# x1's scratch with 264 rows a channel, and the lifted operand loaded as four transfers of 24 partitions

## The reference

```
x = x + L0(gn(x))      # gn: group norm, 4 groups of 2 channels
x = x + L1(gn(x))
L0: 3x3 conv of 8 channels (centre tap masked) -> 32, relu, 1x1 conv -> 8
L1 (per group of 2 channels):
    h = fc0(concat(x, grid_x, grid_y))            # 1x1, 4 -> 10 per group: "the lift"
    for i in 0..3:
        h = irfft2(W_i * low modes of rfft2(h)) + conv1x1_i(h)
        if i < 3: h = h*sigmoid(softplus(beta_i)*h)/1.1
    h = fc2(swish(fc1(h)))                        # 10 -> 128 -> 2 per group
```

## Time and profile before

| | us |
|---|---|
| median of 3 runs | 23,844.61 |
| range of the 3 runs | 23,821.83 to 23,862.16 |
| the profiled execution | 23,827.96 |
| its span, first to last instruction | 23,826.2 |

### The profile page before, as it was taken

How to read it: one execution, slowest core, us unless ns; L and a number is a source line. 1 busy time by engine, 2 the same in 40 slices (tenths; PEclk the granted TensorE clock), 3 DMA queues, 4 the chain that set the end, 5 groups by cost and what they waited for, 6 DMA issues and landing times.

```text
span 23826.2 us, 590215 instructions
## 1 busy us (share of the span) xinstructions
PE 18081.9 (76%) x252434; PEld 7868.4 (33%) x252434; DVE 4542.3 (19%) x8917; ACT 13087.9 (55%) x16068; POOL 45.0 (0%) x69
## 2 busy tenths in 40 slices
PE   4787777787777877778777877777777778877778
PEld 2233332233332333333333333332333323333223
DVE  2111221112211122111121111211112211122111
ACT  2565445664455654556545655456554556544566
POOL 0000000000000000000000000000000000000000
PEclk8888888898888988889888888888888889888889
DMA  4333443334433344433444334443344433344333
GB/s 147 96 88 126 141 140 106 92 113 141 140 109 101 103 140 140 122 93 103 136 140 134 87 99 134 138 141 91 89 133 139 142 100 88 123 142 140 108 92 111
DMA packets 1497569, 2829.48 MB, mean 119 GB/s; under 512 B 126470, under 2 KB 395742, under 8 KB 1466986
## 3 DMA queue, kind: packets, MB, share of 16 engines
q1 hardware_dynamic: 1492353, 2789.18, 38.3%
q10 hardware_dynamic: 2408, 0.28, 0.0%
HBM read 1547.46 MB, written 1241.52 MB: 117 GB/s over the span
## 4 chain that ended last, share of the span: by engine, by line
PE 41%; DMA 26%; ACT 19%; DVE 7%; issue 5%; SPq 2%; ACTq 0%; DVEq 0%
PE PS L600 20%; ACT arena L705 18%; DMA h_d<-hmem 16%; DMA arena<-h_d 5%; DVE gst L904 4%; PE PS L498 4%; DMA hmem<-x_d 3%; PE PS L565 3%; PE PS L469 3%; PE PS L509 3%; PE PS L560 3%; PE PS L519 2%; DMA x_d<-arena 2%; PE PS L478 1%; PE PS L533 1%
## 5 line engine op out<-in xcount | busy, mean ns | idle before, releaser
L705 ACT ACTIVATE arena<-PS 128x1024 f32<-128x1024 f32 x8448 | 8186.8, 1021 | 1404.7 <-PE PS L600 1404.7
L600 PE MATMUL PS<-hmem,f1w 31*128 31x512 f32 x33792 | 4838.7, 642 | 541.9 <-DVE hmem L941 42.2
L613 PE MATMUL PS<-arena,f2w 128*32 128x512 f32 x33792 | 4511.4, 606 | 32.9 <-ACT arena L705 32.9
L565 PE MATMUL PS<-invc,gst 24*32 24x256 f32 x90112 | 3075.9, 421 | 218.4 <-issue 215.1
L698 ACT ACTIVATE hmem<-PS 128x2048 f32<-128x2048 f32 x1056 | 1982.8, 1878 | 1606.9 <-PE PS L565 1606.9
L600 PEld LDWEIGHTS PS<-hmem,f1w 31*128 31x128 f32 x33792 | 1327.0, 183 | 4312.1 <-ACT arena L705 4254.7
L498 PE MATMUL PS<-arena,fwdr 128*32 128x256 f32 x15360 | 1243.3, 450 | 1984.0 <-DMA arena<-h_d 1982.7
L666 ACT ACTIVATE arena<-PS 128x256 f32<-128x256 f32 x1024 | 392.4, 383 | 3956.3 <-PE PS L498 3956.3
L565 PEld LDWEIGHTS PS<-invc,gst 24*32 24x32 f32 x90112 | 2125.0, 144 | 1118.9 <-issue 890.1
L560 PE MATMUL PS<-hmem,mix 30*32 30x512 f32 x33792 | 1817.7, 657 | 440.8 <-DVE gst L904 347.8
L677 ACT ACTIVATE gst<-PS 24x264 f32<-24x264 f32 x2560 | 973.0, 380 | 1436.8 <-PE PS L533 1378.4
(11 more groups left out here) (105 smaller groups left out, 7605.1 us busy)
## 6 DMA issues: line engine op xcount, KB each, us to landing
arena<-h_d SPq DMA_DIRECT2D x960, 1024.0 KB, 6.8
h_d<-hmem SPq DMA_DIRECT2D x1408, 512.0 KB, 3.6
h_d<-hmem SPq DMA_DIRECT2D x1408, 256.0 KB, 4.0
shifted<-in_x SPq DMA_DIRECT2D x990, 128.0 KB
wspec<-in_spec_w SPq DMA_DIRECT2D x97, 1200.0 KB, 5.2
arena<-in_x SPq DMA_DIRECT2D x528, 128.0 KB, 2.5
x_d<-arena SPq DMA_DIRECT2D x512, 128.0 KB, 4.4
hmem<-x_d SPq DMA_DIRECT2D x128, 512.0 KB, 6.7
```

Of the source, the lines that this page charges most:

```text
L565: mm = nc.tensor.matmul(PS[32 * s:32 * s + 32, at + r, y * W:y * W + W], gst[32 * r:32 * r + MODES, s, :, 2 * u + y], invc[32 * r:32 * r + ...
L600: mm = nc.tensor.matmul(PS[:, 2 * ((2 * p + n) % 3) + r % 2, :], f1w[32 * r:32 * r + 31, k, g, :], hmem[32 * r:32 * r + 31, g * PART + u * ...
L613: mm = nc.tensor.matmul(PS[32 * c:32 * c + 32, 6 + u % 2, :], f2w[:, k, g, :], act[p % 2][:, c * ROW2:c * ROW2 + ROW2], start=kg == 0, sto ...
L705: nc.scalar.activation(act[p % 2][:, 1024 * n:1024 * n + 1024], PS[:, bank:bank + 2, :].rearrange("p a b -> p (a b)"), ACT.Silu).then_inc( ...
```

## The change

The scratch `x1_d` gets 264 rows a channel, so that 3 blocks of 88 rows fill it exactly. Rows 256 to 263 are cleared once, by one transfer of 8 partitions by 8 KB in the setup. With that, block k of channel ch begins at a fixed distance of 88 rows from the one before, over channels too. Chunk c of all 24 (channel, block) pairs is one transfer of 24 partitions by 22 rows, and the order within a partition group of 32 becomes channel first, block second (partition 32c + 3ch + k). All four are issued behind the second halves of the row images; no lift load is left between the stores.

The lift's weights in `liftt` are loaded in the new order of rows (three strided loads and one for the rest in place of one). The partitions of `lifted` now belong to other groups than those of the two layouts, so `gm` gets a third layout, each `group_sum` a third matmul, and POOL's power works on three columns. On DVE the two additions of EPS become one over three columns, and `lift_mean` is taken before POOL's power and not after. Addresses of the stores, the row images and the residuals use the new channel pitch (`X1_CH`).

```diff
-    to = np.stack([g, np.arange(128) // 32])
+    to = np.stack([g, np.arange(128) // 32, np.arange(128) % 32 // (NBLK * SC)])
...
-        x1_d = nc.dram_tensor("x1_d", [C, H, W], F32, kind="Internal")
+        x1_d = nc.dram_tensor("x1_d", [C, NBLK * KROWS, W], F32, kind="Internal")
...
-        LIFTED = 16 * (BLOCKS + 4)
+        LIFTED = 16 * (4 + 4)
+        X1_CH = NBLK * KROWS * W
...
-                  (liftt, lift_t[:, 0:32]), (liftb, lift_b), (lg, lift_g), (gridm, gridf), (mixb, mix_b),
+                  (liftt[:, CH - 16:32], lift_t[:, CH - 16:32]),
+                  *[(liftt[:, k:CH - 16:NBLK], lift_t[:, C * k:C * k + C]) for k in range(NBLK)], (liftb, lift_b), (lg, lift_g), (gridm, gridf), (mixb, mix_b),
...
-                def lift_rows(blocks):
-                    for c, k in blocks:
-                        p, n = 32 * c + C * k, kept(c, k, 0, PU)
-                        sp_.dma_start(lifted[p:p + C, 0:n * W], bass.AP(x1_d, (KROWS * k + YY * c) * W, [[PIX, C], [1, n * W]])
-                                      ).then_inc(s_lift, 16)
...
-                upper = [(c, k) for k in range(NBLK) for c in range(4) if KROWS * k + YY * c + YY <= H // 2]
                 for u in range(UNITS):
                     sp_.wait_ge(s_x1, i * UNITS + (u + 1 + HEAD_X1))
                     for t in (2 * u, 2 * u + 1):
-                        sp_.dma_start(combed(x1_d, NQ * t * W, NQ), xt[:, t * W:t * W + W]).then_inc(s_x1st[t // UNITS], 16)
+                        sp_.dma_start(combed(x1_d, NQ * t * W, NQ, X1_CH), xt[:, t * W:t * W + W]).then_inc(s_x1st[t // UNITS], 16)
                     if u == 4:
                         sp_.wait_ge(s_x1st[0], i * (16 * UNITS) + 16 * UNITS)
                         first_images(0)
-                        lift_rows(upper)
                 sp_.wait_ge(s_x1st[1], i * (16 * UNITS) + 16 * UNITS)
                 first_images(1)
-                lift_rows([(c, k) for k in range(NBLK) for c in range(4) if (c, k) not in upper])
+                for c in range(4):
+                    sp_.dma_start(lifted[32 * c:32 * c + NBLK * C, :], bass.AP(x1_d, YY * c * W, [[KROWS * W, NBLK * C], [1, PART]])
+                                  ).then_inc(s_lift, 16)
...
             sp_.wait_ge(s_set, SETUP_V)
+            sp_.dma_start(bass.AP(x1_d, PIX, [[X1_CH, C], [1, X1_CH - PIX]]), lifted[0:C, 0:X1_CH - PIX]).then_inc(s_pad, 16)
             for n in range(PARTS):
                 load(0, n)
+            sp_.wait_ge(s_pad, 16)
...
-                for layout in range(2):
+                for layout in range(3):
                     mm = nc.tensor.matmul(gnps[n][:, 2 * layout + r:2 * layout + r + 1], gm[:, layout, :], mv[:, 3 * r:3 * r + 1],
...
                 if n:
                     V.tensor_scalar(spectral_shift, gnps[n][:, 2:3], -1.0, None, ALU.mult)
-                    V.tensor_scalar(spectral_var, gnps[n][:, 3:4], EPS, None, ALU.add)
-                V.tensor_scalar(mv[:, 6:7], gnps[n][:, 1:2], EPS, None, ALU.add)
+                    V.tensor_scalar(lift_mean, gnps[n][:, 4:5], inside[:, 1:2], None, ALU.mult)
+                V.tensor_scalar(variances, gnps[n][:, 1:6:2], EPS, None, ALU.add)
                 V.drain().then_inc(s_var, 1)
                 dve.wait_ge(s_rstd, nth + 1)
                 if n:
-                    V.tensor_scalar(lift_mean, mean, inside[:, 1:2], None, ALU.mult)
-                    V.tensor_scalar(lift_rstd, rstd, inside[:, 1:2], inside[:, 2:3], ALU.mult, ALU.add)
+                    V.tensor_scalar(lift_rstd, row_rstd, inside[:, 1:2], inside[:, 2:3], ALU.mult, ALU.add)
...
-                nc.gpsimd.tensor_tensor(mv[:, 8:10], mv[:, 6:8], power[:, :], ALU.pow).then_inc(s_rstd, 1)
+                nc.gpsimd.tensor_tensor(rstds, variances, power[:, :], ALU.pow).then_inc(s_rstd, 1)
```

More of the change, by code:

```diff
@@ L178, in program @@
         mix13 = sb("mix13", [128, 2, 32]); mix2 = sb("mix2", [128, G, 32])
-        power = sb("power", [128, 2])
+        power = sb("power", [128, 3])
         beta = sb("beta", [128, 12]); sp = sb("sp", [128, 12]); spt = sb("spt", [128, 12]); rsp = sb("rsp", [128, 12])
@@ L184, in program @@
         invr = sb("invr", [128, 2, NBLK * 4 * YY]); invc = sb("invc", [128, W])
-        gm = sb("gm", [128, 2, 128]); inside = sb("inside", [128, 3]); flat = sb("flat", [128, 4 * KY])
-        stats = sb("stats", [128, CHUNKS, 6]); mv = sb("mv", [128, 13])
+        gm = sb("gm", [128, 3, 128]); inside = sb("inside", [128, 3]); flat = sb("flat", [128, 4 * KY])
+        stats = sb("stats", [128, CHUNKS, 6]); mv = sb("mv", [128, 15])
         ot = sb("ot", [128, 2, 12, 32])
         PS = ctx.enter_context(nc.psum_tensor("PS", [128, 8, 512], F32))
-        gnps = [PS[:, 7, 0:4], PS[:, 3, 0:4]]
-        mean, spectral_var, rstd, spectral_rstd = mv[:, 2:3], mv[:, 7:8], mv[:, 8:9], mv[:, 9:10]
-        spectral_shift, lift_mean, lift_rstd = mv[:, 10:11], mv[:, 11:12], mv[:, 12:13]
+        gnps = [PS[:, 7, 0:6], PS[:, 3, 0:6]]
+        mean, variances, rstds = mv[:, 2:3], mv[:, 6:9], mv[:, 9:12]
+        rstd, spectral_rstd, row_rstd = mv[:, 9:10], mv[:, 10:11], mv[:, 11:12]
+        spectral_shift, lift_mean, lift_rstd = mv[:, 12:13], mv[:, 13:14], mv[:, 14:15]
         s_w = sem("weights_loaded"); s_set = sem("setup_vector"); s_sact = sem("setup_scalar")
@@ L210, in program @@
         s_fc1 = sem("fc1_done"); s_silu = sem("silu_done"); s_fc2 = sem("fc2_done")
-        s_pace = sem("store_admitted"); s_xr = [sem(f"residual{n}_loaded") for n in range(2)]; s_fo = sem("result_ready"); s_out = sem("result_stored")
+        s_pace = sem("store_admitted"); s_pad = sem("rows_below_cleared"); s_xr = [sem(f"residual{n}_loaded") for n in range(2)]; s_fo = sem("result_ready"); s_out = sem("result_stored")
         HEAD_MM2, HEAD_X1, HEAD_OUT, HEAD_FO = 2, 2, 1, 2
@@ L276, in program, with combed @@
         block = ctx.enter_context(nc.Block())
-        def combed(dram, start, rows):
-            return bass.AP(dram, start, [[W, rows], [PIX, C], [1, W]])
+        def combed(dram, start, rows, channel=PIX):
+            return bass.AP(dram, start, [[W, rows], [channel, C], [1, W]])
         @block.sync
@@ L284, in _ @@
             for dst, src in consts:
-                sp_.dma_start(dst, src).then_inc(s_w, 16)
+                sp_.dma_start(dst, src, allow_slow_non_contiguous=True).then_inc(s_w, 16)
             sp_.dma_start(wspec[:, :], spec_w[0, :, :]).then_inc(s_wsp, 16)
@@ L333, in image @@
                     sp_.dma_start(lifted[32 * c + 24:32 * c + 28, :], grid[4 * c:4 * c + 4, :]).then_inc(s_lift, 16)
-                def lift_rows(blocks):
-                    for c, k in blocks:
-                        p, n = 32 * c + C * k, kept(c, k, 0, PU)
-                        sp_.dma_start(lifted[p:p + C, 0:n * W], bass.AP(x1_d, (KROWS * k + YY * c) * W, [[PIX, C], [1, n * W]])
-                                      ).then_inc(s_lift, 16)
                 def first_images(t):
                     for n in range(SC):
-                        sp_.dma_start(himg0[n][64 * t:64 * t + 64], bass.AP(x1_d, n * PIX + t * (PIX // 2),
-                                                                            [[ROW2, 64], [SC * PIX, G], [1, ROW2]])
+                        sp_.dma_start(himg0[n][64 * t:64 * t + 64], bass.AP(x1_d, n * X1_CH + t * (PIX // 2),
+                                                                            [[ROW2, 64], [SC * X1_CH, G], [1, ROW2]])
                                       ).then_inc(s_himg[n], 16)
-                upper = [(c, k) for k in range(NBLK) for c in range(4) if KROWS * k + YY * c + YY <= H // 2]
                 for u in range(UNITS):
@@ L387, in image, with rows_of @@
                                       ).then_inc(s_himg[c % 3], 16)
-                def rows_of(dram, start, c, k, a, n):
-                    return bass.AP(dram, start + (KROWS * k + YY * c + 2 * a) * W, [[PIX, C], [1, n * W]])
+                def rows_of(dram, start, channel, c, k, a, n):
+                    return bass.AP(dram, start + (KROWS * k + YY * c + 2 * a) * W, [[channel, C], [1, n * W]])
                 def residual(q):
@@ L397, in residual @@
                             if n > 0:
-                                sp_.dma_start(xo[q % 2][p:p + C, 0:n * W], rows_of(x1_d, 0, c, k, a, n)).then_inc(s_xr[q % 2], 16)
+                                sp_.dma_start(xo[q % 2][p:p + C, 0:n * W], rows_of(x1_d, 0, X1_CH, c, k, a, n)).then_inc(s_xr[q % 2], 16)
                 def store(q):
@@ L406, in store @@
                             if n > 0:
-                                sp_.dma_start(rows_of(out, i * (C * PIX), c, k, a, n), xo[q % 2][p:p + C, 0:n * W]
+                                sp_.dma_start(rows_of(out, i * (C * PIX), PIX, c, k, a, n), xo[q % 2][p:p + C, 0:n * W]
                                               ).then_inc(s_out, 16)
```

## The result

| | median of the runs, us | ratio to before, 95% interval |
|---|---|---|
| before | 23,839.93 (4 runs) | |
| changed kernel | 23,268.50 (4 runs) | 0.9759 (0.9742 to 0.9776) |

A forecast was written before the change was run, and what follows sets the result against it. It took two transfer waits, the last x1 store and the last lift load, as the bound: 10.7 + 7.9 - 0.5 = 18.1 us an image, 578 us after 1 for setup, giving 23,250 us from 23,828 (range 23,140 to 23,470).

The forecast's parts named there:

- Stores freed: Last x1 stores, no longer behind lift loads, land in 3.5 us (bounds 2.5 and 6.1): 10.7 us an image gained.
- Rate by the partitions reached: Lift loads: rate grows with partitions reached, 164 GB/s for 24 against 55 for 8, so four take 13.1 us.
- Rival B: Lift loads: rate goes by rows per DMA engine, four take 26.2 us; 23,669 us in all; chance 0.09.
- Rival C: Lift loads of 24 partitions no faster than of 8: 39.4 us at 55 GB/s; 24,091 us in all; chance 0.05.
- Rival A: Lift load wholly hidden, landing before the mixed modes: 20.7 us an image gained, 23,167 us in all; chance 0.10.
- D: x1 stores stay late for another cause and the lift gain is given back: no change; chance 0.03.
- Lag of the operand: Lifted operand's arrival after the last x1 store has landed: 20.6 us instead of 28.5, 7.9 us an image gained.
- R: The moment in each image at which the last x1 store has landed; later times are counted from it.
- Group sums: One more matmul in each group sum, about 0.26 us; the two in the feed-forward part cost 0.5 us an image.
- From DVE's normalising on, every step keeps its length.: After the lifted operand arrives, no step changes length, so the pixel products move earlier by the whole sum.
- the first term: Gain from x1 stores landing earlier, 10.7 us an image of the 18.1 forecast.
- The extra matmuls: Third matmul in the group sums: 0.5 us once in the setup, 0.5 us an image in the feed-forward part.

The follow-up runs named there:

- order-only kernel: Kernel before with all twelve 8-partition lift loads issued behind the row images' second halves, none ahead of the last x1 stores: 23,980.12 us, 1.0043 of before.
- 12-partition kernel: Changed kernel with each lift load of 24 partitions cut into two of 12, same bytes, places and order: 23,676.46 us, 0.9915 of before.
- lean ahead of the loop: Changed kernel with the two group sums ahead of the image loop reduced to one layout, and DVE's addition split: 0.9727 of before.
- third-layout kernel: Kernel before with only the third layout of the group-mean table added, loads and order untouched: 23,954.90 us, 1.0029 of before.
- pitch-only: Kernel before with only x1's scratch at 264 rows a channel and addresses adapted: 23,881.82 us, 0.9995 of before.
- lean: Changed kernel with every group sum making only the layouts that are read, and DVE's addition over those columns: 23,227.49 us, 0.9718 of before.
- both-edits: Changed kernel with the lifted operand loaded and normalised in two parts by columns, and group sums making only the layouts read: 23,105.23 us, 0.9673 of before.

## Why the prediction was right, step by step

- *Stores freed.* Right, sized a little low: 11.8 us an image against 10.7, just above the upper bound of 11.7. I took 3.5 us to landing from stores in other traffic; these land in 2.4, below the lower bound of 2.5 taken from four stores. The order-only kernel shows the same 2.4, so the order does this by itself.
- *Rate by the partitions reached.* Right: 154 GB/s against 164 for 24 partitions. With 55 for 8 neighbours, 88 for 12 neighbours and 115 for 8 that are spread, the four shapes order as the ports do that the Trainium skill counts ("SBUF — State Buffer", section "Door 1: The DMA port swizzle"). By it 8 neighbours reach two ports, 12 reach three and 24 reach six; the eight spread rows reach six too, but two of the six take two rows each. Its 27.2 GB/s a port would make 54, 82 and 163 for the contiguous ones, an estimate from that page; the measured 55, 88 and 154 agree within 8%.
- *Rival B* (by engines and rows) fell with the 12-partition kernel: twice the loads of half the rows, and 1.75 times the time rather than the same. *Rival C* (24 partitions no faster than 8 neighbours) fell with the 154 GB/s; what it would have cost the order-only kernel shows, where all twelve loads stand behind the images at the old rate, and which is slower, as C had it. *Rival A* was short by 3.7 us of wait an image. *D* is refuted by the 2.4 us.
- *Lag of the operand.* R+28.5 to R+20.6 forecast, 7.9 us; 7.8 measured (29.05 to 21.28). Both ends were set 0.6 to 0.7 us too early and that cancelled: the first added one image's mixed modes (R+18.0, the mean is R+18.6) to the mean wait, and the second took 164 GB/s for 154. So the wait for the operand is 3.7 us and not 2.6. The 0.95 us that the transforms gained is no gain of its own, since the operand is last: where the mixed modes came 1.8 us later (lean ahead of the loop, R+19.4), the wait was 1.7 shorter.
- *Group sums.* 0.5 us an image forecast in the feed-forward part, where the stage mean grew by 0.67. That mean is no clean measure: the third-layout kernel has 350.5 us there, no more than the order-only and pitch-only kernels of its group with the old sums (350.5 and 350.8). PE's timeline shows the cost itself:

```profile
891.76 1.06 PE L613 MATMUL PS<-arena,f2w 128*32 128x512 f32 x8
892.75 0.83 PE L449 MATMUL PS<-mv,gm 128*128 128x1 f32 x6
...
894.58 1.06 PE L613 MATMUL PS<-arena,f2w 128*32 128x512 f32 x8
```

  The step with the sum is 894.58 - 891.76 = 2.82 us, 0.22 longer than in the earlier trace rows and 0.57 over the usual 2.25. Two such steps make 0.44 us an image, and the forecast was right.
- *"From DVE's normalising on, every step keeps its length."* The step that failed. The layer-0 pixels grew by 1.76 us an image, 56 in all. It hid because the first term was low by 1.1: 18.1 forecast, 17.2 measured. That the time came within 0.1% of the forecast is luck to that extent; the two large terms were right by mechanism.
- *The extra matmuls* were costed by their own time alone, 0.5 us once for those ahead of the loop. That they shift what stands behind them was left out. The runs show that the stage's length changes with the PE instructions ahead of it although its work doesn't: 1.5 us an image between 0 and 16. That PE waits there for its own instructions is a reading, which the grid of the idles and the transfers behind them bear out. The idle named "issue" before L560 and L565 together is 337.0 us in total before, 345.0, 342.5 and 345.1 in the lean-ahead, lean and both-edits kernels, and 386.5 in the changed kernel; L565 alone doesn't part them (258.7 in the lean kernel, 261.0 in the changed one). Why the same idles cost more at one place than at another, and whether a shift between 0 and 12 or beyond 64 would be good, no run shows.

## What to carry to other kernels

A load of few neighbouring partitions with long rows was slow for itself here (55 GB/s) and held up the stores behind it in the queue (14.2 us to landing for the last, 2.4 without); lay the scratch out so that one transfer reaches many partitions, and only then move it behind the stores, since the order alone lost 0.4%. Cut such an operand by when it is used: the first half early took away the wait of 3.7 us that was left. After an edit that adds instructions, compare the stages behind it as well, also those that it doesn't touch.

## What was not expected of the hardware

- A few PE instructions more ahead of an unrolled stage go with a longer stage: 41.2 to 42.1 us in the eight kernels that had 12 to 64 more, 39.6 to 40.1 in the six that had none. Taking sixteen out of the changed kernel ahead of its loop, the eight added ones and eight old ones, made the stage 1.5 us an image shorter. PE's unexplained idles in that stage stand some 256 instructions apart, on a grid fixed in the program.
- A transfer of 12 long rows into 12 neighbouring partitions takes nearly as long as one of 24 into 24 (24.7 us for eight against 14.1 for four, 3.1 and 3.5 each), and one of 8 rows spread over 24 partitions half the time of 8 in neighbouring ones.
